# Two cross attentions over 6404 context rows: heads within query halves, 64-row mask and score products, rounds of two units

## The reference

```
scores = einsum('bhqd,bhkd->bhqk', Q, K) / sqrt(8)
scores = where(mask[:, None] == 0, -1e9, scores)      # layer 2; layer 3: where(context_mask, -inf, attn)
attn   = softmax(scores, axis=-1)
Z      = einsum('bhqk,bhkd->bhqd', attn, V)
```

## Time and profile before

| | us |
|---|---|
| median of 3 runs | 6183.48 |
| span of the profiled execution (the profile gives no other time of it) | 6180.5 |
| TensorE busy | 4319.4 (70%) |
| VectorE busy | 3667.5 (59%) |
| ScalarE busy | 2628.5 (43%) |
| GpSimd busy | 756.9 (12%) |
| exp, L1480, both stages | 1734.3 |
| VectorE with mask, L1515 | 1049.1 |
| VectorE without mask, L1510 | 956.2 |

### The profile page before, as it was taken

The page is one execution under the profiler, slowest core; times in us unless marked ns, Lnnn a source line. Parts: engine busy times, 40 slices in busy tenths (PEclk is TensorE's granted clock), DMA queues, the critical chain, the costliest instruction groups (busy, mean ns, idle before and its releaser), DMA issues. The chain is left out here.

```text
span 6180.5 us, 82959 instructions
## 1 busy us (share of the span) xinstructions
PE 4319.4 (70%) x31970; PEld 1559.0 (25%) x31970; DVE 3667.5 (59%) x7693; ACT 2628.5 (43%) x4771; POOL 756.9 (12%) x842
## 2 busy tenths in 40 slices
PE   5956999544699999999964899999877641134224
PEld 2333444333122222222242122222134320012011
DVE  5464666556877777777345998998724650137122
ACT  2522666224366666666611587888730110001001
POOL 0000000002000000000002000000000027722772
PEclk9878999767799999999976899999988875567567
DMA  0020000024000000000004001100014000000000
GB/s 13 1 62 10 15 11 9 15 100 155 18 12 10 3 12 12 12 12 1 1 6 104 1 12 19 17 12 12 1 15 147 13 5 13 12 5 5 13 13 8
DMA packets 119874, 141.87 MB, mean 23 GB/s; under 512 B 48269, under 2 KB 96620, under 8 KB 116846
## 3 DMA queue, kind: packets, MB, share of 16 engines
q1 hardware_dynamic: 77870, 118.15, 7.6%
q0 software_dynamic: 20480, 10.53, 1.1%
q10 hardware_dynamic: 21128, 7.88, 0.5%
HBM read 103.35 MB, written 33.14 MB: 22 GB/s over the span
## 5 line engine op out<-in xcount | busy, mean ns | idle before, releaser
L1480 ACT ACTIVATE probs<-ps 128x512 f32<-128x512 f32 x3264 | 1734.3, 598 | 763.0 <-PE ps L1425 762.9
L1515 DVE CUSTOM_DVE_ANT_0 junk<-ps,mask 128x512 bf16<-128x512 f32 (+1 forms) x1664 | 1049.1, 678 | 362.5 <-PE ps L1387 346.4
L1510 DVE TENSOR_REDUCE maxima<-ps 128x2 f32<-128x1024 f32 (+1 forms) x832 | 956.2, 1199 | 110.6 <-PE ps L1387 104.2
L1441 PE MATMUL ps<-probs,vstack 128*9 128x512 f32 x6528 | 873.0, 596 | 0.4 <-ACT probs L1480 0.4
L1425 PE MATMUL ps<-qturned,kturned 52*128 52x512 bf16 x3264 | 792.8, 385 | 83.7 <-ACT probs L1480 64.8
L1387 PE MATMUL ps<-kturned,qturned 49*128 49x512 bf16 (+1 forms) x3328 | 704.6, 392 | 110.8 <-DVE maxima L1510 35.7
L3172 POOL DMA_INDIRECT line<-table,index x640 | 644.8, 1008 | 876.9 <-DVE index L3545 483.5
L1418 PE MATMUL ps<-maskT,lower 128*128 128x512 fp8e5 x1632 | 562.3, 387 | 63.5 <-ACT probs L1480 15.1
L1425 PEld LDWEIGHTS ps<-qturned,kturned 52*128 52x128 bf16 x3264 | 196.2, 93 | 791.8 <-ACT probs L1480 462.1
L1387 PEld LDWEIGHTS ps<-kturned,qturned 49*128 49x128 bf16 x3328 | 166.3, 95 | 492.7 <-DVE maxima L1510 200.3
L1418 PEld LDWEIGHTS ps<-maskT,lower 128*128 128x128 bf16 x1632 | 123.5, 96 | 598.6 <-ACT probs L1480 433.4
(11 more groups left out here) (718 smaller groups left out, 4826.6 us busy)
## 6 DMA issues: line engine op xcount, KB each, us to landing
raw<-in_mask_BxSxS_if SPq DMA_DIRECT2D x8, 3202.0 KB, 13.2
kturned<-keys_parts SPq DMA_DIRECT2D x192, 102.0 KB
table<-lines SPq DMA_DIRECT2D x51, 256.0 KB, 3.0
line<-table,index POOLq DMA_INDIRECT x640
keys_parts<-parts SPq DMA_DIRECT2D x24, 384.0 KB, 2.7
vstack<-values_heads SPq DMA_DIRECT2D x16, 459.0 KB, 16.5
lose<-in_mask_SxS_bc SPq DMA_DIRECT2D x32, 128.0 KB
values_heads<-vall SPq DMA_DIRECT2D x2, 1728.0 KB, 10.4
```

The lines of the kernel that those rows point to most:

```text
L1441: last = nc.tensor.matmul(k.ps[at:at + HD + 1, 3, :], vstack[:, p % 2, a, t, :], probs[:, (h * KT + t) % slots, a, :], start=(t < 2), stop ...
L1480: nc.scalar.activation(probs[:, u % slots, a, :], k.ps[:, (2 * u + a) % 3, :], ACT.Exp, scale=(1.0 if maskT is None else 1.0 / STEP8)).the ...
L1510: nc.vector.tensor_reduce(dst, ring(e).rearrange("p (a n) -> p a n", a=2)[:, :, 0:hi - lo], AX.X, ALU.max).then_inc(ring_free[at % 2], 1)
L1515: nc.vector.tensor_tensor_reduce(junk[:, at % 2, a * BANK:a * BANK + hi - lo], ring(e)[:, a * BANK:a * BANK + hi - lo], mask8[:, 4 * b + m ...
```

## The change

- **Order of the halves**: all eight pairs for the first 512 queries, then all for the second. Keys are loaded for each half, in two parts (3072 and 3456 columns), the values with them.
- **Units**: one score bank holds 64 context rows of both heads. Four products of 52 rows by 64 outputs (two heads, two row halves) fill a unit's two banks; there are four score banks for two units, and exp takes 1024 columns at once. In `vstack` each head has its own 9 of 18 columns, the other 9 are zero, so that weigh still needs four products per two units. GpSimd writes these zeros in the context stage, and `values_heads` is twice as long.
- **Mask**: bf16, for one half (`maskT`); the other is kept in DRAM and loaded when half 8 begins. A mask product has 64 rows (`split`, an identity twice side by side).
- **Rounds**: `programme` gives two units per round: masks of both, scores of both, pieces, a weigh, pieces.
- **Pieces**: one head, one bank; the ring is banks 5 to 7, bank 4 is weigh's. Both layers use the VectorE operation of L1515; without a mask it reads a tile of zeros, `nothing`.
- **Shift**: 12 pieces of the half after next are run early, and the shift's turning stands after the fourth of them.

```
 def programme():
...
+    for h in range(HALVES):
+        parts = both_of(h + 1, LEAD, n) if h + 1 < HALVES else []
+        if h + 2 < HALVES:
+            parts += [[("queries", h + 2)]] + both_of(h + 2, 0, 4) + [[("shifted", h + 1)]] + both_of(h + 2, 4, LEAD)
...
+    for g in range(HALVES * KT // 2):
+        out += [("scores", 2 * g)] + spread[2 * g] + late.pop(g, []) + spread[2 * g + 1]
...
 def ring(e):
-            return k.ps[:, 4 + 2 * (ring_at[e] % 2):6 + 2 * (ring_at[e] % 2), :].rearrange("p a b -> p (a b)")
+            return k.ps[:, 5 + ring_at[e] % RING, :]
...
+            def masks(u):
+                h, t = divmod(u, KT)
+                if u >= 2:
+                    pe.wait_ge(probs_ready, u - 1)
+                if h == PAIRS and t % KEPT == 0:
+                    pe.wait_ge(masks_loaded[t // KEPT], 16)
+                for first in range(2):
+                    mine = slice(64 * first, 64 * first + 64)
+                    nc.tensor.matmul(k.ps[:, 2 * (u % 2) + first, :], k.split[mine, :], maskT[mine, t, :],
+                                     start=True, stop=False, skip_group_check=True)
+            def score(u):
...
+                for first in range(2):
+                    for a in range(2):
+                        rows = slice(a * SLOT, a * SLOT + ROWS)
+                        to = slice(64 * (a ^ first), 64 * (a ^ first) + 64)
+                        last = nc.tensor.matmul(k.ps[to, 2 * (u % 2) + first, :],
+                                                kturned[rows, h % 2, t * P + 64 * first:t * P + 64 * first + 64],
+                                                qturned[rows, h % 3, :], start=maskT is None, stop=True, skip_group_check=True)
+                last.then_inc(scores_filled, 1)
...
-                    nc.scalar.activation(probs[:, u % slots, a, :], k.ps[:, (2 * u + a) % 3, :], ACT.Exp,
+                        nc.scalar.activation(probs[:, u % slots].rearrange("p b n -> p (b n)"),
+                                             k.ps[:, bank:bank + 2, :].rearrange("p b n -> p (b n)"), ACT.Exp,
...
-                    nc.vector.tensor_reduce(dst, ring(e).rearrange("p (a n) -> p a n", a=2)[:, :, 0:hi - lo], AX.X,
-                                            ALU.max).then_inc(ring_free[at % 2], 1)
+                lost = nothing[:, 0:hi - lo] if mask8 is None else mask8[:, 4 * b + m, lo:hi].bitcast(mybir.dt.uint8)
+                nc.vector.tensor_tensor_reduce(junk[:, at % RING, 0:hi - lo], ring(e)[:, 0:hi - lo], lost, 1.0, -3.0e38,
+                                               ALU.subtract, ALU.max, maxima[:, h % 2, 4 * a + m, c:c + 1]).then_inc(ring_free[at % RING], 1)
...
+            for h in range(2, HALVES):                       # SyncE, cross
+                sp.wait_ge(scores_filled, (h - 2) * KT + EARLY)
+                keys(h, 0)
+                if h == PAIRS + 1 and maskT is not None:
+                    for a in range(0, KT, KEPT):
+                        last = min(a + KEPT, KT)
+                        sp.wait_ge(scores_filled, (PAIRS - 1) * KT + last)
+                        sp.dma_start(maskT[:, a:last, :]..., k.mask_dram[:, a:last, :]...).then_inc(masks_loaded[a // KEPT], 16)
+                sp.wait_ge(scores_filled, (h - 1) * KT)
+                keys(h, 1)
+                sp.wait_ge(weighed, WEIGHS * (h - 1))
+                values(h)
...
+                if g < 4:                                    # GpSimd, context_sides
+                    for a in range(2):
+                        nc.gpsimd.memset(vall[:, 2 * g:2 * g + 2, a, :, 1 - a, :], 0.0).then_inc(strips_cleared, 1)
```

More of the change, by code:

```diff
@@ L1223, with both_of, programme @@
 CHUNKS = [(a, min(a + BANK, SP)) for a in range(0, SP, BANK)]
-LEAD = 3
+LEAD = 12
 WEIGHS = KT // 2 + 1
+RING = 3
+PAIR = 2 * (HD + 1)
+KEPT = 10
+EARLY = 24
 def pieces():
-    return [(m, c) for m in range(4) for c in range(len(CHUNKS))]
-def programme(lag, masked):
-    n = len(pieces())
[L1236 to L1242, removed]
+    early = [c for c in range(len(CHUNKS)) if CHUNKS[c][1] <= EARLY * P]
+    rest = [c for c in range(len(CHUNKS)) if c not in early]
+    return [(m, c, a) for cs in (early, rest) for m in range(4) for c in cs for a in range(2)]
+def both_of(h, first, last):
+    return [[("piece", h, i), ("piece", h, i + 1)] for i in range(first, last, 2)]
+def programme():
+    n = len(pieces())
+    out = [("queries", 0)] + [("piece", 0, i) for i in range(n)] + [("queries", 1)]
+    out += [("piece", 1, i) for i in range(4)] + [("shifted", 0)] + [("piece", 1, i) for i in range(4, LEAD)]
+    spread = []
+    for h in range(HALVES):
+        parts = both_of(h + 1, LEAD, n) if h + 1 < HALVES else []
+        if h + 2 < HALVES:
+            parts += [[("queries", h + 2)]] + both_of(h + 2, 0, 4) + [[("shifted", h + 1)]] + both_of(h + 2, 4, LEAD)
+        elif h + 1 < HALVES:
+            parts += [[("shifted", h + 1)]]
+        cut = [-(-len(parts) * min(t, KT - 2) // (KT - 2)) for t in range(KT + 1)]
+        spread += [[e for part in parts[cut[t]:cut[t + 1]] for e in part] for t in range(KT)]
     late = {}
@@ L1382, in piece @@
+                if CHUNKS[c][0] == EARLY * P and m == a == 0:
+                    pe.wait_ge(keys_loaded[h % 2][1], 192 * (h // 2 + 1))
                 ring_wait(pe, e)
-                t = 4 * b + m
                 lo, hi = CHUNKS[c]
-                for a in range(2):
-                    rows = slice(a * SLOT, a * SLOT + SHIFT)
-                    last = nc.tensor.matmul(ring(e)[:, a * BANK:a * BANK + hi - lo], qturned[rows, par, t * P:(t + 1) * P],
-                                            kturned[rows, par, lo:hi], start=True, stop=True)
@@ L1389, in piece @@
[L1389 to L1403 removed]
+                rows = slice(a * SLOT, a * SLOT + SHIFT)
@@ L1623, in mask_turned @@
     nc = k.nc
-    groups = [(t, range(a, min(a + 4, KT))) for t in range(NT) for a in range(0, KT, 4)]
+    fours = [range(a, min(a + 4, KT)) for a in range(0, KT, 4)]
+    groups = [(b, m, cs) for b in (1, 0) for cs in fours for m in range(4)]
     with Stage(nc) as s:
+        later = s.sb("later", [P, KT, BANK], BF16)
         turned = s.sem("turned")
@@ L1637, in _ @@
         def _(pe):
-            for i, (t, cs) in enumerate(groups):
+            for i, (b, m, cs) in enumerate(groups):
                 if i >= NBANK:
```

326 lines of the change are left out of this document (159 added, 167 removed).

## The result

The changed kernel takes 5975.87 us (median of 4, 5964.89 to 5977.03) against 6184.24 (4 runs, 6180.24 to 6186.04): ratio 0.9661, 95% interval 0.9647 to 0.9675, 208 us faster. The forecast was 5873. The result lies outside the forecast's own range (5825 to 5925) and inside the wide one (5815 to 6035). The profiled run is the lowest of the four, 5964.89, with a span of 5962.8.

A forecast was written before the change was run, and what follows sets the result against it. Masked rounds were taken as bound by a TensorE-ScalarE chain, unmasked bodies by VectorE (90% busy). Masked -298.5, unmasked -36.5, context +40, starts -18, rest +3 make -310: 6183.5 to 5873 us; own range 5825 to 5925, wide 5815 to 6035.

The forecast's parts named there:

- A: Rival: a unit's four score products go in two steps, masked +114, unmasked +42 us, total 6029; chance 0.15.
- B: Rival: exp gains nothing from 1024 columns, masked chain +0.34 a round, total 6020; chance 0.08.
- Masked chain, 2.75: Masked body: a round of two units takes 2.75 us through ScalarE's exps; 408 rounds make 1122.
- D: Rival: quarter products run one behind the other, masked round 3.90, unmasked 3.47, slower than before at 6705; chance 0.04.
- Extras, 35: Masked stage: copies, sums, transposes and rounds with five or six pieces add 35 us, bounds 8 and 55.
- Unmasked half, 65.9: Unmasked body: VectorE bounds each half at 65.9 us, against 67.6 before; fifteen halves 989.
- my own mark of 67.6: Sign set beforehand: the forecast is wrong if an unmasked half takes over 67.6 us.
- rival C: Three single banks starve VectorE by 0.25 at two visits per round: unmasked +191, masked +78, total 6142; chance 0.10.
- Context +40: Context stages: doubled value strips, with GpSimd's clears and longer stores, add 20 us each, twice; bounds 10 and 60 for both.
- Starts -18: Start of each cross stage: first piece 11 us after first key transfer, not 20; -9 each, bounds 0 and -22.
- Heads: Start of each cross stage, maxima of the first half alone: 72.5 us each, against 68 before in the masked stage.
- The transfers beside the rounds: Keys and values loaded per half, priced at nothing with their cover; +70 us if that cover fails.

The follow-up runs named there:

- dealing by weight: Changed kernel with pieces, turnings, third weighs and sums dealt so each round gets the same weight, and the shift turned behind the eighth piece: 5905.63 us, ratio 0.9558.
- by pairs: The kernel dealt by weight, with its pieces dealt in pairs again: 5900.11 us, ratio 0.9542.
- the even kernel: Changed kernel with pieces dealt one by one instead of in pairs, up to a half's last unit: 5958.26 us, ratio 0.9643.

## Why the prediction was right in kind and 103 us off

The mechanism came as told; the sum missed by what the rounds add above a clean one. That the result still lies in the wide range is in part luck: its upper part was kept for rivals A and B, and neither came.

- **Masked chain, 2.75**: right, 2.775 in clean rounds. 408 x 0.025 = 10 of the miss. Rivals A, B and D are refuted by the scores' 0.56 for eight and the exp's 1.022.
- **Extras, 35 (bounds 8 to 55)**: this step failed. 103 was measured, 68 more. I priced rounds with five or six pieces and the sums by what they came to before the change, and two things were wrong. The first is the yardstick: "1460 - 1452 = 8" takes the round of 3.56 for clean, while the median round was 3.45 and the extras in the body 53. The second is the carrying over. Before, a six-piece round of three visits cost 0.3 and there were 34; here it costs 1.0 and there are 63. Six visits take VectorE 3.66, the ring holds three, and TensorE stops in front of the weigh and the scores that ScalarE needs. The experiments bear it out: dealing by weight and moving the queries takes 47 us out of the masked excess with the same work. No run changes the size of the ring itself.
- **Unmasked half, 65.9**: failed by my own mark of 67.6: 1043 / 15 = 69.5. VectorE's visits were summed over a half (its busy time of 973 bears the sum out), as if what a light round leaves free could be used in a heavy one. It can't: two pieces still make the round 2.1, six make it 3.65. The body is 54 us over its forecast and the tail 5; dealing by weight gave back 15 of them (26 by pairs), with a head per bank and plain maxima 31. Some 68 us of excess remain in that version, and no run says how much of it a better order could take.
- **Ring of three, rival C** (0.25 at each visit): no; clean rounds are 2.484. The ring costs in crowded rounds only.
- **Context +40**: +15 measured. Strips were taken at 1.9 ns per element from a clearing in single elements; in runs of nine it is 1.05.
- **Starts -18**: -26, the first piece comes 6.7 us after the first key transfer and not 11. Heads 143 against 145. The transfers beside the rounds cost nothing, as said.
- **Sum against the profiled run**: from its first piece to its last weigh the masked stage got 219 us shorter and not 298.5, +79.5; the unmasked one 21 longer and not 36.5 shorter, +57; context -25, starts -8, clock in unchanged code -12, small stages +1. Together +92.5, where 5962.8 lies 92 over (6180.5 - 310). The median of 5975.87 lies 103 over its forecast of 5873; the profiled run is the fastest of its four.

## What to carry to other kernels

An engine's work divided by the number of rounds is a bound only if every round has the same work. Where rounds are bound by different engines and the buffer between them holds less than one round's work, price the fullest round by itself: its visits times their length, less the clean round. Here that is 6 x 0.61 - 2.775 = 0.9 masked (measured 1.0) and 6 x 0.61 - 2.484 = 1.2 unmasked (measured 1.2), and the program's own list gives their number, 63 per layer. Check the clean round too: one round read from a trace is no median. And look at what stands directly behind a step that another engine must answer: one piece right behind the turning of its own queries cost 38 us of excess in 28 halves.

## What the chip showed that I had not expected

- The quarter products: four of 52 rows by 64 outputs side by side in the time of one, though two share their rows: eight in 0.56.
- A change of product shape costs 0.10 to 0.12 in most places (0.32 from a pair of pieces to the weigh, 0.215 of it stream), but not in all: from pieces (49 rows by 128 outputs) to masks (64 by 128) it is 0.22 to 0.23, from pieces to scores of 52 by 128, in the kernel before, 0.22. With masks of 128 rows it is 0.32 again.
- GpSimd clears 918 elements in runs of nine in 0.96 us; 816 single ones with a stride took 1.57.
- Inside a dense body TensorE's wait of 2.02 us came with a fall to 1.2 GHz in 11 of 14 cases of the even kernel. In the changed kernel the same masked round stands at six halves' ends, with TensorE's waits of 0.52 and 0.58 in and before it: three times the clock fell (0.57 from 1768 to 1772 for one, the round 6.28 long) and three times not (1.00 from 1922.7 to 1927.4, the round 4.64). Two equal rounds can thus differ by 1.6 us with nothing in the program to tell them apart.
